# Two graph-attention layers: when the accumulator sums may start, where they stand against the mask extraction, and when a maximum is spread

## The chip, the core and the metric

The kernel runs on one core of a Trainium2 chip. The metric is device time in microseconds (us) from start to end of one execution, and the time of a kernel is the median of several runs. The engines of the core are TensorE (PE), VectorE (DVE), ScalarE (ACT), GpSimd (POOL) and SyncE (SP). Each works through its own instructions in the order in which they are written, and engines wait for one another with semaphores: an instruction adds to a semaphore when it is done, and another engine waits until the count has reached a value. A waiting instruction holds back all that stands behind it on its engine.

## The reference

Two layers of graph attention over 4096 nodes with 64 features, each with a residual and a layer norm. `adj` is a 4096 x 4096 matrix of 0 and 1.

```python
def _L0_gnn_ref(h, adj, a):
    src, dst = h @ a[:D, 0], h @ a[D:, 0]
    e = src[:, None] + dst[None, :]
    e = jnp.where(e > 0, e, 0.01 * e)
    attention = softmax(jnp.where(adj > 0, e, NEG_INF), axis=1)
    return attention @ h

def _L1_gnn_ref(h, adj, W, a):
    Wh = h @ W
    e = leaky_relu((Wh @ a1)[:, None] + (Wh @ a2)[None, :], 0.2)
    attention = softmax(jnp.where(adj > 0, e, NEG_INF), axis=1)
    return elu(attention @ Wh)

x = _layernorm(x + _L0_gnn_ref(x, adj, L0_gnn_a))
x = _layernorm(x + _L1_gnn_ref(x, adj, L1_gnn_W, L1_gnn_a))
```

## The kernel before

Since the exponential of a leaky ReLU of s + d is a product of a factor of the row and a factor of the column on either side of s + d = 0, the kernel never forms the scores. It forms two 0/1 matrices, "edge and s + d > 0" (`pos`) and "edge and s + d < 0" (`neg`), and multiplies each by weighted values (`wmov`). The row's factors are applied to the sums afterwards.

**Tiling.** Each layer goes over 8 supertiles q of 512 rows, each of 4 tiles t of 128 rows. Inside a supertile stand 8 steps k, each over 512 columns in 4 blocks. I write (layer, q, k) for a step, so (1,3,0) is the first step of supertile 3 of layer 1. One step passes through four engines:

- ACT, `compare` (L666): four instructions write the signs of s + d for the step into `neg`, one of 4 buffers.
- DVE, `negative` (L827) and `positive` (L838): bitwise operations with the mask `mask_t` make `neg` and `pos`. There are 2 buffers of `pos`.
- PE, `products` (L1215): 32 matmuls, 8 for each tile t, that add into the accumulator `acc[t]` in PSUM. They wait for `positive` of the step. In the middle of a step, after tile 1, stands what the function `between` issues.
- In layer 0 the mask must first be made: PE transposes a piece of the loaded `adj` into `tb` (L1139, in `between`, two steps ahead), and DVE extracts it from there (`extract`, L753, one step ahead). The transpose for a later step waits until `tb` is extracted. Layer 1 uses the same masks again. The pieces of `adj` are loaded by DMAs that POOL issues, each when its buffer has been transposed.

**The end of a supertile.** After step 7 the four accumulators are read by `sum_parts` (DVE, L853): four reductions, one for each tile, into `part`. They stand behind `positive` of step 0 of the next supertile. Sum t waits until PE has finished tile t (`acc_ready`, for the last tile `mm_done`). The first product of step 0 into `acc[t]` waits for sum t (`acc_free`). Then the epilogue runs on POOL: two instructions (L341, L343) multiply `part` by the row factors, and these two are the only ones that read `part`. The rest (L346 to L417) works in `num`, `tmp` and small columns up to the write of `xout` (L417). On its way it needs DVE twice (a reciprocal; `take_stats`, L867 and L871) and in layer 1 ACT once (`elu`, L647, an exponential that stands behind the signs of step 5). `pdone[layer]` counts its instructions, `EPI` = 13 in layer 0 and 17 in layer 1 for each supertile. In layer 1 `take_stats` stands ahead of `negative` of step 7, so the epilogue ends shortly before the next supertile's sums.

**The sums' wait.** `sum_parts` waits until the whole epilogue of the supertile before has counted (L845, L847). It guards `part`, which the new sums overwrite.

**The maximum.** In (0,6) the maximum of the column terms of layer 1 is spread to all partitions: DVE takes it over columns (`find_max`, L761), PE transposes it (`turn_stat`, L1155), DVE takes it over the row (`spread_max`, L766), PE spreads it (`spread_stat`, L1159), and DVE copies it (`take_max`, L778) and centres the column terms (`centre`, L772). From these ACT makes exponentials (L601, L602, behind the signs of step 3), from which POOL makes the first weights of layer 1 (L328, written behind its epilogue's step 2 work), and DVE and ACT finish them in (0,6) and (0,7). Both PE instructions stand ahead of the products of (0,6,1).

The loops over q: supertiles 0, 1, 6 and 7 of each layer are written out, 2 to 5 run in a hardware loop of two supertiles a turn.

## Time and profile before

| | |
|---|---|
| median of 3 runs | 445.18 us (444.62 to 447.87) |
| the profiled execution, whole | 445.9 us |
| its span, first to last instruction | 444.3 us |
| PE busy | 409.0 us, 92% |
| ACT busy | 383.4 us, 86% |
| DVE busy | 379.6 us, 85% |
| POOL busy | 252.9 us, 57% |

The span is one execution seen by the profiler. Layer 0 fills it up to about 243 us, layer 1 the rest. The engines are busy for 85% and more each, so the shares tell little of which one sets the pace. That must be read at the places where one waits for another.

### The profile page before, as it was taken

To read this page: it belongs to the slowest core of one execution; us is meant where nothing else is said; L and a number is where in the kernel's file an instruction comes from. 1 tells how busy PE (TensorE), PEld (TensorE's weight loads), DVE (VectorE), ACT (ScalarE), POOL (GpSimd) and SP (SyncE) were. 2 spreads that over 40 slices of the span, in tenths; PEclk is the share of its full clock that TensorE was granted. 3 is DMA by queue.
4 is the path that set the end of the run, shared out by engine and by line. 5 is a ranking of instruction groups with operands and counts; after the bars stand their busy time and mean duration, and the time that the engine had idled before them with its cause. 6 is when DMAs were issued, how large, how long until landed. Compare 5 with 4: busy or idle time off the path is not lost.

```text
span 444.3 us, 11835 instructions
## 1 busy us (share of the span) xinstructions
PE 409.0 (92%) x4484; PEld 396.8 (89%) x4484; DVE 379.6 (85%) x682; ACT 383.4 (86%) x590; POOL 252.9 (57%) x293
## 2 busy tenths in 40 slices
PE   1599999999999999999998989999999999999990
PEld 1388899999999999999998989999998999999980
DVE  4799898898989989889899988689898989898963
ACT  3898897979979798797998989999999898989930
POOL 5533263763737547295492135567786959595930
PEclk9999999999999999999999999999999999999995
DMA  5999979799897998989510000000000000000000
GB/s 114 97 107 107 90 68 96 63 101 84 74 101 60 98 88 70 88 73 87 78 52 1 1 25 2 1 25 2 26 1 25 0 24 0 24 1 24 3 25 16
DMA packets 22766, 22.48 MB, mean 51 GB/s; under 512 B 1344, under 2 KB 22464, under 8 KB 22720
## 3 DMA queue, kind: packets, MB, share of 16 engines
q0 software_dynamic: 17424, 16.78, 43.5%
q1 hardware_dynamic: 4208, 4.05, 2.8%
q10 hardware_dynamic: 1088, 1.05, 0.7%
q8 instruction: 28, 0.46, 0.4%
q14 instruction: 18, 0.15, 0.1%
HBM read 69.30 MB, written 2.10 MB: 161 GB/s over the span
## 4 chain that ended last, share of the span: by engine, by line
PE 40%; DVE 28%; issue 12%; ACT 9%; POOL 5%; DMA 3%; DVEq 1%; POOLq 0%; ACTq 0%
PE acc L1215 34%; DVE neg L827 9%; ACT neg L666 9%; PE tb L1139 5%; DVE odd L738 5%; DVE pos L838 3%; DVE scr L853 3%; POOL small L403 2%; DVE mask_t L753 2%; DMA enc<-in_adj 2%; DVE split L810 1%; DMA mask_t<-in_x 1%; POOL scr L404 1%; DVE mask_t L810 1%; DVE bst L867 1%
## 5 line engine op out<-in xcount | busy, mean ns | idle before, releaser
L1215 PE MATMUL acc<-wmov,pos 128*128 128x195 bf16 x2016 | 358.6, 248 | 7.7 <-DVE scr L853 3.3
L666 ACT ACTIVATE neg<-srcb,dcol 128x512 int8<-128x512 f32 x512 | 357.5, 959 | 4.6 <-PE acc L1215 4.4
L1215 PE MATMUL acc<-wmov,neg 128*128 128x195 bf16 x2016 | 358.7, 249 | 0.0
L1215 PEld LDWEIGHTS acc<-wmov,pos 128*128 128x128 fp8e4 x2016 | 198.5, 98 | 15.6 <-issue 8.1
L1215 PEld LDWEIGHTS acc<-wmov,neg 128*128 128x128 fp8e4 x2016 | 197.5, 98 | 2.3 <-issue 1.3
L838 DVE TENSOR_TENSOR pos<-neg,mask_t 128x1024 uint16<-128x1024 uint16 x128 | 104.6, 817 | 14.0 <-PE acc L1215 0.9
L827 DVE TENSOR_TENSOR neg<-neg,mask_t 128x1024 uint16<-128x1024 uint16 x128 | 105.8, 827 | 11.8 <-ACT neg L666 8.9
L486 POOL DMA_DIRECT2D enc<-in_adj x31 | 24.7, 798 | 63.4 <-PE tb L1139 60.1
L753 DVE TENSOR_SCALAR mask_t<-tb 128x512 uint32<-128x512 uint32 (+1 forms) x64 | 43.8, 685 | 10.0 <-PE tb L1139 10.0
L1139 PE MATMUL tb<-ident,enc 128*128 128x128 f32 x256 | 39.3, 277 | 3.8 <-DMA enc<-in_adj 3.8
L738 DVE SCALAR_TENSOR_TENSOR odd<-mask_t,odd 128x1024 uint32<-128x1024 uint32 x32 | 38.8, 1213 | 0.0
L341 POOL TENSOR_TENSOR scr<-scr,acol 128x260 f32<-128x260 f32 x14 | 13.7, 976 | 38.1 <-DVE scr L853 38.1
L853 DVE TENSOR_REDUCE scr<-acc 128x130 f32<-128x390 f32 x60 | 29.7, 555 | 6.5 <-POOL xout L417 6.3
L1139 PEld LDWEIGHTS tb<-ident,enc 128*128 128x128 f32 x256 | 28.9, 142 | 4.5 <-DMA enc<-in_adj 4.0
L403 POOL TENSOR_TENSOR small<-small 128x4 f32<-128x4 f32 x14 | 19.4, 1383 | 1.2
L400 POOL TENSOR_SCALAR small<-mv 128x4 f32<-128x4 f32 x14 | 9.1, 652 | 19.1 <-DVE mv L871 18.9
L343 POOL TENSOR_TENSOR scr<-scr,acol 128x260 f32<-128x260 f32 x14 | 14.9, 1064 | 0.0
L328 POOL TENSOR_TENSOR split<-val,bcol 128x520 f32<-128x520 f32 x8 | 9.2, 1155 | 8.4 <-ACT bcol L602 7.8
L631 ACT COPY xt<-pg 128x256 f32<-128x256 f32 x8 | 3.0, 369 | 12.6 <-PE pg L1175 12.6
L362 POOL TENSOR_TENSOR scr<-scr 128x256 f32<-128x256 f32 x14 | 12.9, 920 | 1.1
L346 POOL TENSOR_TENSOR scr<-scr 128x260 f32<-128x260 f32 x14 | 12.7, 907 | 1.1
L417 POOL TENSOR_TENSOR xout<-scr,small 128x256 f32<-128x256 f32 x14 | 12.5, 889 | 1.1
(138 smaller groups left out, 300.5 us busy)
## 6 DMA issues: line engine op xcount, KB each, us to landing
enc<-in_adj POOLq DMA_DIRECT2D x31, 512.0 KB, 8.4
mask_t<-in_x ACTq DMA_DIRECT2D x4, 256.0 KB, 6.0
x_rows<-xout SPq DMA_DIRECT2D x8, 128.0 KB, 3.9
resid<-x_rows SPq DMA_DIRECT2D x8, 128.0 KB, 2.1
out<-xout SPq DMA_DIRECT2D x8, 128.0 KB, 1.7
wmov<-mask_t SPq DMA_DIRECT2D x2, 390.0 KB, 3.9
enc<-in_adj POOLq DMA_DIRECT2D x2, 256.0 KB, 8.6
resid<-in_a SPq DMA_DIRECT2D x1, 64.0 KB, 4.6
```

The source lines that it names most:

```text
L341: ops.tensor_tensor(num, part[:, :, 0, :], wide(acol[:, layer, 0, q, :], FD), ALU.mult)\
L343: ops.tensor_tensor(tmp, part[:, :, 1, :], wide(acol[:, layer, 1, q, :], FD), ALU.mult)\
L403: ops.tensor_tensor(rstd, var, mhalf, ALU.pow).then_inc(done, 1)
L486: nc.gpsimd.dma_start(enc8[:, u, :, :], adj_v[q, u]).then_inc(adj_landed[u], 16)
L666: ins = nc.scalar.activation(neg[:, k % SR, :, b], srcb[:, q % 2, :], ACT.Sign, bias=dcol[:, layer, c:c + 1])
L738: nc.vector.scalar_tensor_tensor(odd[:, :], mask_pairs[:, n, :], NOT_BINARY, odd[:, :], ALU.bitwise_and, ALU.bitwise_or).then_inc(looked, 1)
L753: nc.vector.tensor_scalar(mask_t[:, q, k, :, :], tb[:, :, :].bitcast(U32), WORD, None, ALU.bitwise_and).then_inc(masked, 1)
L827: nc.vector.tensor_tensor(neg16[:, k % SR, :], neg16[:, k % SR, :], bits, ALU.bitwise_and)\
L838: nc.vector.tensor_tensor(pos16[:, k % MR, :], neg16[:, k % SR, :], bits, ALU.bitwise_xor)\
L853: nc.vector.tensor_reduce(part[:, t, :, :], acc[t][:, 0:2 * WC].rearrange("p (s r c) -> p s c r", s=2, r=SPLIT), AX.X, ALU.add).then_inc(a ...
L1139: ins = nc.tensor.transpose(tb[:, t, :], enc[:, k // KP, t, k % KP * P:(k % KP + 1) * P], ident[:, :])
L1215: ins = nc.tensor.matmul(acc[t][:, side * WC:(side + 1) * WC], m[:, t * P:(t + 1) * P, b], wmov[:, c, side * WC:(side + 1) * WC], start=fi ...
```

## The change

Four edits, in one diff:

- The sums of a supertile no longer wait for the whole epilogue of the one before, but for its first two instructions (count + 2). In its place the epilogue's first instruction gets the wait for the end of the epilogue before. That epilogue runs on the same engine, but for the last supertile of layer 0, whose epilogue runs on DVE.
- `sum_parts` can do a part of the tiles. In the general body the sums of tiles 0 and 1 stand ahead of `extract` for the next step, and those of tiles 2 and 3 behind it. In layer 1 there is no `extract`, so that the four follow one another as before.
- `take_max` and `centre` in (0,6) move from step 1 to step 2 on DVE.
- `spread_stat` on PE moves from ahead of the products of (0,6,1) into their middle, behind the transposes.

```diff
@@ epilogue_sums
+            if layer == 1 and is_first(q):
+                eng.wait_ge(pdone[0], EPI[0] * NQ)
+            elif later(q):
+                eng.wait_ge(done, base)
             eng.wait_ge(acc_free, TI * (Q + 1))
@@ sum_parts
-            def sum_parts(layer, q, Q):
+            def sum_parts(layer, q, Q, tiles=range(TI)):
                 if layer == 1 and is_first(q):
-                    dve.wait_ge(pdone[0], EPI[0] * NQ)
+                    dve.wait_ge(pdone[0], EPI[0] * (NQ - 1) + 2)
                 elif later(q):
-                    dve.wait_ge(pdone[layer], EPI[layer] * q)
-                for t in range(TI):
+                    dve.wait_ge(pdone[layer], EPI[layer] * (q - 1) + 2)
+                for t in tiles:
@@ DVE body
                     negative(layer, q, k)
                     positive(layer, q, k)
+                    if done is not None and k == 0:
+                        sum_parts(*done, range(0, TI // 2))
                     if ahead(layer, q, k, 1):
                         extract(*ahead(layer, q, k, 1))
                     if done is not None and k == 0:
-                        sum_parts(*done)
+                        sum_parts(*done, range(TI // 2, TI))
@@ DVE body, layer 0, last but one supertile
                         if k == 1:
                             spread_max(1)
+                        if k == 2:
                             take_max(1)
                             centre(1, 0, NB * EARLY)
@@ PE between()
+                        if layer == 0 and is_last_but_one(q) and k == 1:
+                            spread_stat(1)
@@ PE body, ahead of products(0, 6, 1)
                         pe.wait_ge(grp_set, 3 * EARLY)
                         turn_stat(1)
-                        spread_stat(1)
```

How the order moves on DVE at the start of supertile (0,6), from its step 0 to the centring. The kernel before:

```order
L838 TENSOR_TENSOR pos<-neg,mask_t 128x1024 [waits negs,mm_done]
L753 TENSOR_SCALAR mask_t<-tb 128x512 [waits turned]
L853 TENSOR_REDUCE scr<-acc 128x130 [waits acc_ready,pdone0]
L853 TENSOR_REDUCE scr<-acc 128x130 [waits acc_ready] x2
L853 TENSOR_REDUCE scr<-acc 128x130 [waits mm_done]
L761 TENSOR_REDUCE stat<-dcol 128x1 [waits grp_set]
L827 TENSOR_TENSOR neg<-neg,mask_t 128x1024 [waits masked,signs]
L838 TENSOR_TENSOR pos<-neg,mask_t 128x1024 [waits negs,mm_done]
L753 TENSOR_SCALAR mask_t<-tb 128x512 [waits turned]
L766 TENSOR_REDUCE gst<-pg 1x1 [waits stat_turned]
L778 COPY cmax<-pg 128x1 [waits max_spread]
L772 TENSOR_SCALAR dcen<-dcol,cmax 128x20 [waits cmax_set]
```

The changed kernel at the same place (its lines are numbered a few higher: L857 is L853 of before, L757 is L753, L770 is L766):

```order
L842 TENSOR_TENSOR pos<-neg,mask_t 128x1024 [waits negs,mm_done]
L857 TENSOR_REDUCE scr<-acc 128x130 [waits acc_ready,pdone0]
L857 TENSOR_REDUCE scr<-acc 128x130 [waits acc_ready]
L757 TENSOR_SCALAR mask_t<-tb 128x512 [waits turned]
L857 TENSOR_REDUCE scr<-acc 128x130 [waits acc_ready,pdone0]
L857 TENSOR_REDUCE scr<-acc 128x130 [waits mm_done]
L765 TENSOR_REDUCE stat<-dcol 128x1 [waits grp_set]
L831 TENSOR_TENSOR neg<-neg,mask_t 128x1024 [waits masked,signs]
L842 TENSOR_TENSOR pos<-neg,mask_t 128x1024 [waits negs,mm_done]
L757 TENSOR_SCALAR mask_t<-tb 128x512 [waits turned]
L770 TENSOR_REDUCE gst<-pg 1x1 [waits stat_turned]
```

Two of the four sums have passed the extraction, and the copy of the maximum and the centring are gone from here. They stand one step later, behind the next `positive`, `extract`, the reciprocal and the copy of `scur`.

PE at the start of step (0,6,1), before:

```order
L1155 MATMUL pg<-ident,stat 1x128 [waits stat_set,grp_set]
L1159 MATMUL pg<-gst,ones 128x1 [waits gst_set]
L1215 MATMUL acc<-wmov,pos 128x195 [waits poss]
L1215 MATMUL acc<-wmov,neg 128x195
```

In the changed kernel L1162 (L1155 of before) is followed by the 16 products of tiles 0 and 1 (L1222). Behind them, in the middle of the step, stands this:

```order
L1146 MATMUL tb<-ident,enc 128x128 [waits masked,adj_landed1]
L1146 MATMUL tb<-ident,enc 128x128 x3
L1166 MATMUL pg<-gst,ones 128x1 [waits gst_set]
L1222 MATMUL acc<-wmov,pos 128x195
```

The matmul that spreads the maximum has moved from directly behind the transpose to 16 products and four mask transposes later.

## Rows read from the trace of the kernel before

**Rows 1.** Waits of all engines: who, line, for whom: us, times, longest

```profile
DVE scr L853 <- POOL xout L417: 6.3, 5, 1.3
PE acc L1215 <- DVE scr L853: 3.3, 7, 0.9
```

**Rows 2.** Timeline, PE, layer 1: start us, duration, instruction, [idle before]

```profile
292.60 0.24 PE L1215 MATMUL acc<-wmov,pos 128*128 128x195 bf16 x1
...
312.41 0.25 PE L1215 MATMUL acc<-wmov,pos 128*128 128x195 bf16 x1
...
315.10 0.25 PE L1215 MATMUL acc<-wmov,neg 128*128 128x195 bf16 x1
315.66 0.24 PE L1215 MATMUL acc<-wmov,pos 128*128 128x195 bf16 x1 [0.31 <-DVE scr L853]
...
412.59 0.26 PE L1215 MATMUL acc<-wmov,pos 128*128 128x195 bf16 x1
```

**Rows 3.** Timeline, DVE, supertiles (1,2) and (1,3)

```profile
291.11 2.25 DVE L853 TENSOR_REDUCE scr<-acc 128x130 f32<-128x390 f32 x4
293.28 0.68 DVE L827 TENSOR_TENSOR neg<-neg,mask_t 128x1024 uint16<-128x1024 uint16 x1
...
311.55 0.69 DVE L838 TENSOR_TENSOR pos<-neg,mask_t 128x1024 uint16<-128x1024 uint16 x1
...
314.95 1.98 DVE L853 TENSOR_REDUCE scr<-acc 128x130 f32<-128x390 f32 x4 [1.30 <-POOL xout L417]
316.84 0.68 DVE L827 TENSOR_TENSOR neg<-neg,mask_t 128x1024 uint16<-128x1024 uint16 x1
...
336.58 0.69 DVE L838 TENSOR_TENSOR pos<-neg,mask_t 128x1024 uint16<-128x1024 uint16 x1
```

**Rows 4.** Timeline, POOL, epilogues of (1,1) ending and (1,2) beginning

```profile
314.20 0.61 POOL L417 TENSOR_TENSOR xout<-scr,small 128x256 f32<-128x256 f32 x1
317.00 1.00 POOL L341 TENSOR_TENSOR scr<-scr,acol 128x260 f32<-128x260 f32 x1 [2.19 <-DVE scr L853]
```

**Rows 5.** Timeline, ACT and DVE, step (1,3,6): what the epilogue holds back

```profile
326.26 4.91 ACT L666 ACTIVATE neg<-srcb,dcol 128x512 int8<-128x512 f32 x7
...
329.94 1.22 DVE L827 TENSOR_TENSOR neg<-neg,mask_t 128x1024 uint16<-128x1024 uint16 x1
```

**Rows 6.** Timeline, PE, layer 0: into (0,4) and into (0,6)

```profile
133.56 0.25 PE L1215 MATMUL acc<-wmov,neg 128*128 128x195 bf16 x1
133.93 0.24 PE L1215 MATMUL acc<-wmov,pos 128*128 128x195 bf16 x1
...
187.60 0.25 PE L1215 MATMUL acc<-wmov,neg 128*128 128x195 bf16 x1
187.81 0.24 PE L1215 MATMUL acc<-wmov,pos 128*128 128x195 bf16 x1
```

**Rows 7.** Timeline, DVE, start of supertile (0,6)

```profile
186.50 0.69 DVE L753 TENSOR_SCALAR mask_t<-tb 128x512 uint32<-128x512 uint32 x1 [1.13 <-PE tb L1139]
187.11 1.97 DVE L853 TENSOR_REDUCE scr<-acc 128x130 f32<-128x390 f32 x4
```

**Rows 8.** Timeline, PE, start of step (0,6,1)

```profile
191.01 0.27 PE L1155 MATMUL pg<-ident,stat 128*1 128x128 f32 x1
191.66 0.38 PE L1159 MATMUL pg<-gst,ones 1*128 1x1 f32 x2 [0.37 <-DVE gst L766]
191.97 0.26 PE L1215 MATMUL acc<-wmov,pos 128*128 128x195 bf16 x1
```

**Rows 9.** Timeline, ACT, supertile (0,6): exponentials, signs, and a later wait

```profile
192.53 0.22 ACT L601 ACTIVATE bcol<-dcen 128x20 f32<-128x20 f32 x1 [0.51 <-DVE dcen L772]
...
192.77 5.60 ACT L666 ACTIVATE neg<-srcb,dcol 128x512 int8<-128x512 f32 x8
...
207.47 0.37 ACT L631 COPY xt<-pg 128x256 f32<-128x256 f32 x1 [1.45 <-PE pg L1175]
```

**Rows 10.** Timeline, DVE, `negative` of step (0,6,4)

```profile
198.73 0.66 DVE L827 TENSOR_TENSOR neg<-neg,mask_t 128x1024 uint16<-128x1024 uint16 x1
```

## Prediction

> **What bounds the kernel now.** I read the waits first. Two of them belong together [rows 1]: DVE's sums waited 6.3 us in 5 places for the last instruction of the epilogue, and PE's products waited 3.3 us in 7 places for the sums. The second is small beside 444.3 us, so the question is whether PE is what sets the pace. It is: take PE's timeline of layer 1 [rows 2]. Supertile (1,2) starts its products at 292.60, its step 7 at 312.41, and its last product stands at 315.10. A product follows another at 0.09 (32 in the 2.78 from 312.41 on), so the next supertile could have begun at 315.19. An undisturbed supertile of layer 1 is thus 315.19 - 292.60 = 22.59 us. But (1,3,0) began at 315.66, and the reader sees the sums as its releaser.
>
> How much is lost in all? Without stalls (1,7,1) would begin four supertiles and one step after 315.19: 315.19 + 4 x 22.59 + 2.78 = 408.33. It began at 412.59 [rows 2]. So layer 1 loses 4.26 us between these points, more than the waits view puts down to the sums, because PE also pays at steps 1 and 7, where DVE is late by what it stood idle.
>
> DVE's timeline says why [rows 3]. At (1,2,0) the sums go straight through and take 2.25, stretched by PE, which is not yet done with the last tiles. At (1,3,0) DVE stands for 1.30 until L417 is done, which runs from 314.20 to 314.81 on POOL [rows 4], and only then sums for 1.98. From `negative` of (1,3,1) at 316.84 to the end of `positive` of (1,4,0) at 336.58 + 0.69 = 337.27 DVE has no idle time of note: 20.43 us of work. With the sums (1.98, the next instruction starts 0.09 before their end) this is 22.3 us, and with the 1.3 us of waiting 23.6. So PE could do a supertile in 22.6 and DVE in 22.3, but the wait makes it 23.6.
>
> In layer 0 each boundary has a stall too, another one [rows 6]: into (0,4) PE goes from 133.56 to 133.93, 0.28 more than the pace of 0.09. The cause is order on DVE [rows 7]: the extraction stands ahead of the sums and waits 1.13 us for PE's transposes. The sums start 0.6 us behind its start, and PE's first product 0.70 us after the first sum starts (187.11 to 187.81).
>
> **Part 1, the sums' wait.** The first two instructions of an epilogue start as soon as the sums are done (L341 at 317.00 behind sums that end at 316.93, [rows 3, 4]), so "count + 2" is reached early in a supertile and asked for only at the start of the next. The 1.3 us fall away in all 5 places. Take (1,3,0). Before, sum 0 started at 314.95 and PE at 315.66, 0.71 later. Now sum 0 can start 1.3 to 1.4 us earlier, near 313.6, and PE's tile 0 is free at about 314.3, ahead of 315.19. The last sum must wait for PE's last product, as in (1,2), where `negative` of step 1 follows 0.68 us after the first product (293.28 against 292.60). So DVE is held to PE from there, and every supertile looks like (1,2).
>
> Does DVE then keep up to step 7? In (1,2) it did, with 0.17 to spare: `positive` of step 7 ended at 311.55 + 0.69 = 312.24 and PE used it at 312.41 [rows 2, 3]. The DVE work between is the same in (1,3) to (1,6). This margin is about the hand-over itself, so a tenth may be lost per supertile. I take 4.2 of the 4.26 us. Bounds: nothing less than 3.7, if 0.1 to 0.15 is lost in each of four supertiles; nothing more than 4.3.
>
> What is late next? The wait that moved to POOL costs nothing, since POOL has done L417 itself 2.19 us before L341 may start [rows 4]. The epilogue starts earlier by what the sums gain, and so do the exponential on ACT behind it and the signs of step 6. In (1,3) those signs start at 326.26, four at 0.70 each (4.91 for 7), done about 329.1, and DVE takes them at 329.94 [rows 5]. Set against PE, which gained less than DVE there, the chain keeps some 0.3 to 0.8 us.
>
> One cost no row shows: sums that run beside L404 and L417 on POOL, since they waited for the latter so far. From below it is nothing; from above, if one blocked the other whole, 0.61 us (L417) in 5 places, 3.1 us. I take nothing, since that time would first fill the 2.19 us in which POOL waits. The Trainium skill (SBUF — State Buffer, Who interferes with whom) says that a `tensor_reduce` on this chip never contends with GpSimd for their shared port, but that an operation with two inputs in SBUF blocks or is blocked for the whole of the other. By that rule this cost is nothing and the gain of part 1 stays 4.2, where whole blocking would leave 1.1; no row of before can show it.
>
> **Part 2, two sums ahead of the extraction.** Now sum 0 follows `positive` and no longer waits for the transposes. In (0,6) the extraction idled 1.13 us from 185.37 on, so sum 0 starts near 185.4 and frees tile 0 near 186.1, long before PE is ready (187.60 + 0.09 = 187.69). The stall goes: 0.28 at the starts of (0,2) to (0,5), four times, and 0.12 at (0,6) and at (0,7), where the gap was 0.21 (187.60 to 187.81, [rows 6]). Sum: 4 x 0.28 + 2 x 0.12 = 1.4. The extraction comes behind two sums of 0.47 each. It stood waiting for 1.13 anyway, so it ends at most 0.1 to 0.3 later, and PE wants it only for the transposes in the middle of step 0, 16 products (1.4 us) after its start. At (0,1) DVE works without a break for the next two steps, so PE only stands later: no gain. From below the whole part is worth nothing, if PE's new time is taken by the next late mask or signs; from above 1.4 and some 0.5 at (0,1).
>
> **Part 3, the spreading.** Between (0,6,0) and (0,6,1) PE takes 191.97 - 191.01 = 0.96 us for two tiny matmuls, since the second waits for DVE's maximum [rows 8]. Now the first stays (nothing to its 0.27) and the second comes when its input is long there (nothing to 0.31, from 191.66 to 191.97). I take the middle of each, 0.15: the gain is 0.96 - 0.15 - 0.15 = 0.7, bounds 0.4 to 0.96.
>
> The price is on ACT. The centring comes a step later on DVE. A step takes 3.20 us there (187.81 to 191.01, [rows 6, 8]), and PE and DVE begin it some 0.8 sooner than before, so ACT's exponentials start at 192.53 + 3.2 - 0.8 = 194.9. Queued behind them are the signs of steps 4 and 5, which then start near 195.1 in place of 192.77, 2.3 us later [rows 9]. Queued behind them on DVE is `negative` of step 4, at 198.73 [rows 10]. The signs take 2.8 us (5.60 for 8), so they are done at 197.9, against 198.73 - 0.8 = 197.9 wanted: just hidden, since DVE then waits for transposes anyway. ACT gives the lateness back at its own later waits, 1.45 us ahead of L631 [rows 9] and others. What isn't hidden would be lost, up to some 0.5 us.
>
> **Sum.** 4.2 + 1.4 + 0.7 = 6.3 us, less 0.2 for small hand-overs and the extra register instructions in the loops. The profiled span goes from 444.3 to 438.2. The whole profiled execution took 445.9, 0.7 over the median of 445.18; I take the 6.1 off the median: 439.1.
>
> **Rivals.** Changes below 1%, or 4.45 us, are about what a measurement of this kernel can't tell from none.
>
> - *Layer 0 gives its part back.* The end of layer 0 and the start of layer 1 have stalls of their own, from weights that pass through POOL, ACT and DVE in turn. If one of these chains starts from something not moved by PE, parts 2 and 3 (2.0 us) vanish. For it: ACT is 2.3 us later in (0,6). Against: extraction and ACT's copies there wait for PE [rows 7, 9], so they shift with it. Time 445.18 - 4.1 = 441.1. Chance 0.15.
> - *DVE or the epilogue's chain stays the bound in layer 1.* The margins are 0.17 and 0.3 us. If 0.3 us is lost in each of 5 supertiles, the gain is 4.6 and the time 440.6. Chance 0.13.
> - *The epilogue chain becomes the bound, slower than before.* Place: POOL from L341 to the exponential and the signs of step 6 [rows 4, 5]. The price is what the chain grows by per supertile beyond its 0.3 us, five times. To eat 6.1 it must grow by over 1.5 us each; with 2 us each it would be 5 x 1.7 - 6.1 = 2.4 slower, 447.6. POOL gives no sign of it, since its instructions keep their neighbours on DVE but for the sums. Chance 0.03.
> - *The wait was not what held PE,* and the change does nothing in layer 1: 445.18 - 2.0 = 443.2. Against it stand the 4.26 us with the sums as releaser. Chance 0.05.
>
> The forecast has the rest, 0.64. The low end is all stalls gone, 4.3 + 1.9 + 0.96 = 7.2: 438.0. The high end takes in the first two rivals with a margin: 442.0. Faster by over 1% means below 440.7: the forecast and half of the second rival and a little of the first, 0.74. Slower by over 1%: 0.02. Within 1%: 0.24.
>
> **What would show it.** Sums of (1,3,0) to (1,7,0) without a wait for L417, and starts of PE's supertiles in layer 1 all 22.6 us apart. If they are 22.8 to 23.0 apart, with PE waiting at step 7 for `positive`, DVE is the bound; if DVE waits for signs at step 6, it is the epilogue's chain. In layer 0, no gap ahead of the first product of (0,2) to (0,7), and 0.3 us in place of 0.96 ahead of (0,6,1). If `negative` of (0,6,4) waits for ACT, part 3's price was not hidden. The prediction is wrong if POOL's instructions from L341 on become longer, or if PE's starts in (0,7) and (1,0) have not moved by what (0,6) gained.

## The result and the profile after

| | before | changed |
|---|---|---|
| median of 5 runs each, same chip | 445.26 us (444.62 to 447.87) | 438.74 us (438.66 to 442.47) |
| ratio | | 0.9854, 95% interval 0.9821 to 0.9887 |
| the profiled execution, whole | 445.9 | 442.47 |
| its span | 444.3 | 440.6 |
| PE busy | 409.0, 92% | 408.1, 93% |
| DVE busy | 379.6, 85% | 382.2, 87% |

The changed kernel is faster by 1.5%, 0.4 us under the forecast of 439.1. The profiled execution of the changed kernel happens to be its slowest: it reaches step (0,0,7) 2.2 us later than before does (50.12 us against 47.91), because of a slow stretch near the start that the last section shows. So I compare the two traces from the start of that step on. From there to the start of step (1,7,1) before takes 412.59 - 47.91 = 364.69 us (from the unrounded times), the changed kernel 408.64 - 50.12 = 358.52. That is 6.17 us less, where the forecast's three terms added up to 6.3.

The waits of the changed kernel, as [rows 1] of before (who, line, for whom: us, times, longest):

```profile
DVE scr L857 <- POOL xout L421: 0.2, 1, 0.2
PE acc L1222 <- DVE scr L857: 1.0, 2, 0.7
```

The sums' 6.3 us of waiting for the epilogue have become 0.2, and PE's 3.3 us for the sums 1.0. In the page's chain of what ended last, PE had 40% and DVE 28% in before:

```profile
PE 74%; DVE 12%; issue 5%; DMA 5%; POOL 1%; ACT 1%; DVEq 0%; POOLq 0%
```

PE's timeline of layer 1 (start us, duration, instruction), the first products of (1,2,0), (1,3,0) and (1,7,1), to be read with [rows 2]:

```profile
292.97 0.24 PE L1222 MATMUL acc<-wmov,pos 128*128 128x195 bf16 x1
...
315.56 0.24 PE L1222 MATMUL acc<-wmov,pos 128*128 128x195 bf16 x1
...
408.64 0.25 PE L1222 MATMUL acc<-wmov,pos 128*128 128x195 bf16 x1
```

A supertile takes 315.56 - 292.97 = 22.59 us, and so does each of the five, within 0.02: (1,2,0) to (1,7,1) is 115.67 us against 119.99 in before.

DVE and POOL where (1,3,0) begins, to be read with [rows 3, 4]:

```profile
313.34 0.69 DVE L842 TENSOR_TENSOR pos<-neg,mask_t 128x1024 uint16<-128x1024 uint16 x1
313.95 2.37 DVE L857 TENSOR_REDUCE scr<-acc 128x130 f32<-128x390 f32 x4
```

```profile
314.58 0.61 POOL L421 TENSOR_TENSOR xout<-scr,small 128x256 f32<-128x256 f32 x1
```

The sums start right behind `positive`, while POOL is still in its last instructions, and end 0.76 us after PE has begun the next supertile (316.32 against 315.56): they follow PE now, not POOL.

In layer 0 PE's rows at the start of (0,6) and around (0,6,1), to be read with [rows 6, 8]:

```profile
188.65 0.25 PE L1222 MATMUL acc<-wmov,neg 128*128 128x195 bf16 x1
188.74 0.24 PE L1222 MATMUL acc<-wmov,pos 128*128 128x195 bf16 x1
...
191.94 0.27 PE L1162 MATMUL pg<-ident,stat 128*1 128x128 f32 x1
...
193.96 0.38 PE L1166 MATMUL pg<-gst,ones 1*128 1x1 f32 x2
194.27 0.26 PE L1222 MATMUL acc<-wmov,pos 128*128 128x195 bf16 x1
```

The gap ahead of (0,6,0) is 0.09 us, the plain pace, and ahead of (0,6,1) only the first small matmul is left, 0.11 us (the product behind it starts at 192.05). In the middle of the step the second one holds the products for 0.31 us.

### The profile page after: what moved, and what is told of

Same layout as the page of the kernel before. It is cut to its first block, busy times and chain, and to the rows that moved or that the text cites. A ratio compares the mean times of both kernels' runs of the same rounds, so it can differ in the third digit from the quotient of the medians.

```text
span 440.6 us, 11844 instructions
## 1 busy us (share of the span) xinstructions
PE 408.1 (93%) x4484; PEld 399.5 (91%) x4484; DVE 382.2 (87%) x682; ACT 382.9 (87%) x590; POOL 254.4 (58%) x293
## 4 chain that ended last, share of the span: by engine, by line
PE 74%; DVE 12%; issue 5%; DMA 5%; POOL 1%; ACT 1%; DVEq 0%; POOLq 0%
PE acc L1222 66%; PE tb L1146 5%; DMA enc<-in_adj 3%; DVE neg L831 3%; DVE pos L842 2%; DMA mask_t<-in_x 1%; PE srcb L1156 1%; DVE mask_t L757 1%; DVE mask_t L814 1%; DVE split L814 1%; DVE wmov L820 1%; DVE scr L857 1%; ACT neg L670 1%; PE pg L1190 1%; DVE enc L814 1%
## 5 line engine op out<-in xcount | busy, mean ns | idle before, releaser
L1222 PE MATMUL acc<-wmov,pos 128*128 128x195 bf16 x2016 | 358.8, 249 | 5.0 <-DVE pos L842 3.8
L1222 PE MATMUL acc<-wmov,neg 128*128 128x195 bf16 x2016 | 358.9, 249 | 0.0
L1222 PEld LDWEIGHTS acc<-wmov,pos 128*128 128x128 fp8e4 x2016 | 199.1, 99 | 9.1 <-DVE pos L842 7.1
L1222 PEld LDWEIGHTS acc<-wmov,neg 128*128 128x128 fp8e4 x2016 | 198.1, 98 | 2.4 <-issue 1.3
L842 DVE TENSOR_TENSOR pos<-neg,mask_t 128x1024 uint16<-128x1024 uint16 x128 | 103.5, 809 | 14.1 <-PE acc L1222 0.9
L831 DVE TENSOR_TENSOR neg<-neg,mask_t 128x1024 uint16<-128x1024 uint16 x128 | 103.7, 811 | 11.6 <-ACT neg L670 9.1
L757 DVE TENSOR_SCALAR mask_t<-tb 128x512 uint32<-128x512 uint32 (+1 forms) x64 | 43.9, 686 | 8.2 <-PE tb L1146 7.4
L742 DVE SCALAR_TENSOR_TENSOR odd<-mask_t,odd 128x1024 uint32<-128x1024 uint32 x32 | 38.8, 1212 | 0.0
L857 DVE TENSOR_REDUCE scr<-acc 128x130 f32<-128x390 f32 x60 | 32.2, 558 | 2.0 <-POOL xout L421 0.2
L345 POOL TENSOR_TENSOR scr<-scr,acol 128x260 f32<-128x260 f32 x14 | 13.0, 927 | 30.0 <-issue 23.1
L404 POOL TENSOR_SCALAR small<-mv 128x4 f32<-128x4 f32 x14 | 8.9, 639 | 19.1 <-DVE mv L875 18.9
L328 POOL TENSOR_TENSOR split<-val,bcol 128x520 f32<-128x520 f32 x8 | 9.2, 1156 | 7.9 <-ACT bcol L606 7.8
L366 POOL TENSOR_TENSOR scr<-scr 128x256 f32<-128x256 f32 x14 | 13.1, 936 | 1.1
L374 POOL TENSOR_TENSOR scr<-scr,small 128x256 f32<-128x256 f32 x14 | 11.9, 850 | 2.1 <-DVE small L865 0.5
L421 POOL TENSOR_TENSOR xout<-scr,small 128x256 f32<-128x256 f32 x14 | 12.5, 891 | 1.1
```

The source lines that it names most:

```text
L742: nc.vector.scalar_tensor_tensor(odd[:, :], mask_pairs[:, n, :], NOT_BINARY, odd[:, :], ALU.bitwise_and, ALU.bitwise_or).then_inc(looked, 1)
L757: nc.vector.tensor_scalar(mask_t[:, q, k, :, :], tb[:, :, :].bitcast(U32), WORD, None, ALU.bitwise_and).then_inc(masked, 1)
L831: nc.vector.tensor_tensor(neg16[:, k % SR, :], neg16[:, k % SR, :], bits, ALU.bitwise_and)\
L842: nc.vector.tensor_tensor(pos16[:, k % MR, :], neg16[:, k % SR, :], bits, ALU.bitwise_xor)\
L857: nc.vector.tensor_reduce(part[:, t, :, :], acc[t][:, 0:2 * WC].rearrange("p (s r c) -> p s c r", s=2, r=SPLIT), AX.X, ALU.add).then_inc(a ...
L1222: ins = nc.tensor.matmul(acc[t][:, side * WC:(side + 1) * WC], m[:, t * P:(t + 1) * P, b], wmov[:, c, side * WC:(side + 1) * WC], start=fi ...
```

## The experiments

They ran on three chips in turn, each with its own runs of before: 446.56 us there for the first four kernels, 445.29 for the next four, 445.77 for the last three. A time is compared with its own before. Two traces are compared between the starts of the same steps on PE. These comparisons carry the argument: the runs of before on the first of the chips spread from 445.56 to 448.40 us, and by the medians there the three parts alone would bring 5.0, 2.5 and 0.4 us, more together than the whole change.

**One part at a time.** First the wait alone (edit of `epilogue_sums` and of the two waits in `sum_parts`, with the four sums in one piece):

```diff
-                    dve.wait_ge(pdone[layer], EPI[layer] * q)
+                    dve.wait_ge(pdone[layer], EPI[layer] * (q - 1) + 2)
```

> The kernel before with the sums' wait alone changed (count + 2, and the wait at the epilogue's first instruction); order on DVE and the spreading as before. My theory: it is the cause of nearly all that layer 1 gained, 4.3 us, so about 440.9 against 445.2, and PE's supertiles (1,2) to (1,7) start 22.6 us apart. The rival, that DVE gets its time in layer 1 from the order of the sums or from what layer 0 gained: under 3 us. Layer 0 should keep its gaps of 0.28 and 0.12 us.

Measured: 441.54 us, ratio 0.988 (0.9857 to 0.9903). PE's first product of (1,7,1), where that of (1,2,0) stands at 292.71:

```profile
408.38 0.25 PE L1219 MATMUL acc<-wmov,pos 128*128 128x195 bf16 x1
```

That is 115.67 us, to the hundredth what the changed kernel has, so all of layer 1's gain of 4.32 us is this edit. The starts in layer 0 are spaced as in before. Between (0,0,7) and (1,7,1) this kernel takes 360.40 us, 4.29 less than before.

Then the split of the sums alone, still behind the old wait:

```diff
+                    if done is not None and k == 0:
+                        sum_parts(*done, range(0, TI // 2))
                     if ahead(layer, q, k, 1):
                         extract(*ahead(layer, q, k, 1))
                     if done is not None and k == 0:
-                        sum_parts(*done)
+                        sum_parts(*done, range(TI // 2, TI))
```

> The kernel before with the order alone changed: sums of tiles 0 and 1 ahead of the extraction, 2 and 3 behind it; the old wait for the whole epilogue and the old spreading stay. My theory: 1.4 us, all in layer 0 (0.29 at the starts of (0,2) to (0,5), 0.12 at (0,6) and (0,7)), so about 443.8; nothing at (0,1). Layer 1 keeps its stalls, 4.3 us, with DVE waiting 1.3 us for L417 five times. The rival, that layer 0 gives its part back in (0,7) and (1,0): 445.2.

Measured: 444.1 us, ratio 0.9951 (0.9924 to 0.9978). The gaps ahead of (0,2) to (0,7) are gone on PE, 1.41 us in all. Layer 1's waits stand as they were: the view of the waits gives the first line of [rows 1] again, 6.3 us in 5 places. From (1,2,0) to (1,7,1) PE takes 120.03 us (119.99 in before).

The two parts act in different layers and don't touch each other.

Last the spreading alone:

```diff
+                        if k == 2:
                             take_max(1)
                             centre(1, 0, NB * EARLY)
@@ PE between()
+                        if layer == 0 and is_last_but_one(q) and k == 1:
+                            spread_stat(1)
@@ PE body, ahead of products(0, 6, 1)
-                        spread_stat(1)
```

> The kernel before with the spreading of the maximum alone changed on PE and DVE. My theory from the trace of the changed kernel: 0.84 us are gained ahead of (0,6,1) and 0.40 lost in its middle, so 0.4 to 0.5 us, about 444.8, which is near what can be told from none; the trace should show the two numbers. The rival: ACT's exponentials, now some 2 to 3 us later in (0,6), make the step (0,6,4) late, and it is 0 or a loss.

Measured: 446.12 us, ratio 0.9993 (0.9964 to 1.0022), no change. Its trace explains it. From (0,6,0) to (0,7,0) it takes 27.38 us against 27.82, so 0.44 is gained. From (0,7,0) to the start of layer 1 it takes 29.05 against 28.32, so 0.73 is lost again, more than was gained. I ran this kernel again, to see whether the loss is the luck of one execution:

> The third part alone a second time, in another execution. If the loss of 0.73 us behind (0,7,0), one stall of 2.1 us ahead of the products of (0,7,6), follows from the order and the times of this kernel, it stands there again, and the time is within 0.3 us of the kernel before. If it is the luck of one execution, how DVE and POOL meet, then the stalls at (0,7,5) to (0,7,7) are those of before (0.63, 0.34, 0.85), the way from (0,7,0) to (1,0,0) is 28.3, and the profiled execution is 0.4 below the kernel before at the same points.

Measured: 445.22 us, ratio 0.9987 (0.9969 to 1.0004). Every start on PE from (0,6,0) to (1,0,0) stands where it stood, within 0.01 us: 29.05 again. The loss belongs to the kernel. Rows of this trace, POOL's and then DVE's, from step (0,7,2) (which starts on PE at 220.78) on:

```profile
220.65 1.29 POOL L362 TENSOR_TENSOR scr<-scr 128x256 f32<-128x256 f32 x1
...
227.87 1.15 POOL L404 TENSOR_TENSOR scr<-scr,mv 128x256 f32<-128x256 f32 x1
...
230.00 1.52 POOL L328 TENSOR_TENSOR enc<-val,bcol 128x520 f32<-128x520 f32 x1
231.48 1.07 POOL L328 TENSOR_TENSOR split<-val,bcol 128x520 f32<-128x520 f32 x1
234.58 1.07 POOL L328 TENSOR_TENSOR enc<-val,bcol 128x520 f32<-128x520 f32 x1 [2.03 <-ACT wmov L622]
```

```profile
220.66 0.69 DVE L827 TENSOR_TENSOR neg<-neg,mask_t 128x1024 uint16<-128x1024 uint16 x1
...
227.85 0.70 DVE L816 TENSOR_TENSOR wmov<-split 128x520 bf16<-128x520 f32 x1
...
229.68 0.92 DVE L838 TENSOR_TENSOR pos<-neg,mask_t 128x1024 uint16<-128x1024 uint16 x1
...
231.56 1.55 DVE L810 TENSOR_TENSOR enc<-enc 128x520 f32<-128x520 f32 x1 [0.36 <-POOL enc L328]
...
234.62 1.57 DVE L838 TENSOR_TENSOR pos<-neg,mask_t 128x1024 uint16<-128x1024 uint16 x1
```

And the rows of before at the same instructions (PE starts (0,7,2) at 222.04):

```profile
221.91 0.73 POOL L362 TENSOR_TENSOR scr<-scr 128x256 f32<-128x256 f32 x1
...
228.90 0.61 POOL L404 TENSOR_TENSOR scr<-scr,mv 128x256 f32<-128x256 f32 x1
...
230.51 1.51 POOL L328 TENSOR_TENSOR enc<-val,bcol 128x520 f32<-128x520 f32 x1
```

```profile
221.92 1.27 DVE L827 TENSOR_TENSOR neg<-neg,mask_t 128x1024 uint16<-128x1024 uint16 x1
...
229.10 0.97 DVE L816 TENSOR_TENSOR wmov<-split 128x520 bf16<-128x520 f32 x1
...
231.20 1.37 DVE L838 TENSOR_TENSOR pos<-neg,mask_t 128x1024 uint16<-128x1024 uint16 x1
```

Read them so. At 220.65 a POOL instruction and `negative` on DVE start 0.01 us apart. With part 3 alone DVE runs its 0.69 and POOL takes 1.29. In before POOL ran its 0.73 and DVE took 1.27. Each time one of the two is done in its normal time and the other as if it had waited for the first. Up to L362 POOL stood equally far behind the start of (0,7,0) in both, to 0.01 us. The 0.56 us that L362 takes longer bring about a second meeting: L404 now starts 0.02 us behind `weigh`'s L816 on DVE and takes 1.15, where in before it started 0.20 ahead of it, ran its 0.61, and L816 took the longer time. So POOL reaches the weights' products (L328) 0.74 us later, at 230.00 - 214.38 = 15.62 against 230.51 - 215.63 = 14.88. In before, the first of these lies on `positive` of step 5 and lengthens it (1.37), and PE waits ahead of step 5. With part 3 alone it misses most of that one (0.92), but `weigh` (L810) must wait for it and then runs into the second (1.55), and `positive` of step 6 into the third (1.57, where in before it took 0.69). PE shows the outcome. From the product before to the first product of steps 5, 6 and 7 of (0,7) it takes 0.63, 0.34 and 0.85 us in before and 0.09, 2.08 and 0.39 here, where the pace is 0.09:

```profile
236.25 0.26 PE L1216 MATMUL acc<-wmov,pos 128*128 128x195 bf16 x1 [1.83 <-DVE pos L838]
```

The Trainium skill (SBUF — State Buffer, Who interferes with whom) says that an instruction of DVE with two inputs in SBUF contends with one of GpSimd that reads SBUF, and that who issues first keeps the port for its whole instruction. That one waits for the whole of the other agrees with these traces: 0.69 + 0.61 is about the 1.29. The order agrees for L404 and L816, of which the one that starts first keeps its time in both kernels. For L362 and `negative` the traces can't show it: POOL's recorded start is 3 to 7 ns ahead in all twelve traces that have this meeting, yet DVE is the one lengthened in before and with part 1 alone, and POOL in the ten others, each that has part 2 or part 3. What tips this tie stays open.

**Part 3 inside the change.** Does the changed kernel have this loss? Its way from (0,7,0) to (1,0,0) is 28.33 us, as in before. The same tie stands there (POOL takes 1.29), but L408, the L404 of before, takes 0.60, and L328 starts 14.89 us behind (0,7,0), as in before. The reason is part 2: its sums are done sooner, so the epilogue's chain on POOL stands 0.22 us nearer to the start of (0,7,0) (L366 starts 6.06 behind it, L362 of part 3 alone 6.28). L408 then starts at 13.29, ahead of `weigh` at 13.47, where part 3 alone had it at 13.50, behind. Part 2 alone shows the same 6.06 and 13.29. To see what part 3 is worth there, I took it back out of the changed kernel (the diff of part 3 above, reversed):

> The changed kernel without part 3: the maximum is copied and centred in step 1 of (0,6) again and both small matmuls stand ahead of the products of (0,6,1). My theory, that parts add up: (0,6,0) to (0,7,0) on PE is 0.44 us longer than in the changed kernel (27.82 against 27.38), with 0.96 us between the two first products there and nothing in the middle of step 1; from (0,7,0) to (1,0,0) 28.3 us, as before and as changed; the time is 439.4. Rival, what part 3 gained alone it loses later: (0,7,0) to (1,0,0) is shorter by 0.4 or more, and the time is 438.9 or less.

Measured: 439.14 us, ratio 0.9841 (0.9816 to 0.9866). (0,6,0) to (0,7,0) takes 27.70 us against 27.25 with part 3 (both 0.12 shorter than the figures expected, since the gap ahead of (0,7) is gone in both), and from there to layer 1 28.32. From (0,0,7) to (1,7,1) it takes 359.01 against 358.57 in a second execution of the changed kernel: 0.44 us. So within the change part 3 brings its 0.44 and nothing comes back, by the traces; the timed ratios are too close to tell. Ahead of (0,6,1) the second small matmul has its old wait of 0.37 us for DVE's maximum again.

**The price of the small matmul.** In the changed kernel the spreading matmul is issued twice:

```diff
+                if layer == 1:
+                    nc.tensor.matmul(pg[:, P:P + 1], ones[0:1, 0:1].broadcast_to([1, P]), gst[0:1, 0:1], start=True, stop=True)
                 nc.tensor.matmul(pg[:, P:P + 1], ones[0:1, 0:1].broadcast_to([1, P]), gst[0:1, 0:1], start=True, stop=True)\
```

> The changed kernel with the small matmul that spreads the maximum issued twice in the middle of (0,6,1), the same value to the same place. In the changed kernel it held the next product for 0.31 us. If each such fp32 matmul costs its own time on PE, the hold is near 0.5 to 0.6 us; if the 0.31 is mostly a change from the products to another shape and type and back, the second adds under 0.1 us and the hold is near 0.35 to 0.4. The rest of the kernel is unchanged, so the time moves by no more than 0.3 us.

Measured: 439.84 us in one run, which says little. PE's rows say it:

```profile
191.31 0.38 PE L1167 MATMUL pg<-gst,ones 1*128 1x1 f32 x2
191.55 0.36 PE L1168 MATMUL pg<-gst,ones 1*128 1x1 f32 x2
191.84 0.26 PE L1224 MATMUL acc<-wmov,pos 128*128 128x195 bf16 x1
```

The first takes 0.24 us up to the second, that one 0.29 up to the product: together 0.53 in place of 0.31. The step (0,6,1) is 0.22 us longer. So each such fp32 matmul of a single column costs some 0.22 to 0.24 us of its own, and the change of shape only the rest, under 0.1. This is read from one execution.

**Why half the sums.** In the changed kernel all four sums are put ahead of the extraction:

```diff
                     if done is not None and k == 0:
-                        sum_parts(*done, range(0, TI // 2))
+                        sum_parts(*done)
                     if ahead(layer, q, k, 1):
                         extract(*ahead(layer, q, k, 1))
-                    if done is not None and k == 0:
-                        sum_parts(*done, range(TI // 2, TI))
```

> The changed kernel with all four sums ahead of the extraction, none behind it. The last sum waits for PE's last product, and the extraction behind it would end about 1.3 us after PE's first product of step 0, where PE wants it 1.4 us after. If only the first sums matter to PE, the time is that of the changed kernel, 438.7, within 0.3. The rival, that the halving matters because the extraction becomes late for the transposes: a stall of PE in the middle of step 0 at (0,2) to (0,7), some 0.2 to 0.5 us each, so 440 to 441.5.

Measured: 444.06 us, ratio 0.9939 (0.9911 to 0.9967): most of the gain is gone (2.5 us are left against its own before). DVE's rows around the start of (0,2), which is at 79.37 us on PE, with two sums left out at the top:

```profile
78.88 1.26 DVE L857 TENSOR_REDUCE scr<-acc 128x130 f32<-128x390 f32 x2 [0.56 <-PE acc L1220]
80.05 0.68 DVE L757 TENSOR_SCALAR mask_t<-tb 128x512 uint32 x1
80.95 1.08 DVE L831 TENSOR_TENSOR neg<-neg,mask_t 128x1024 uint16<-128x1024 uint16 x1 [0.21 <-DVE mask_t L757]
82.13 1.04 DVE L842 TENSOR_TENSOR pos<-neg,mask_t 128x1024 uint16<-128x1024 uint16 x1
```

The same place in the changed kernel, where (0,2,0) starts at 81.81:

```profile
80.78 0.69 DVE L757 TENSOR_SCALAR mask_t<-tb 128x512 uint32 x1
81.39 1.18 DVE L857 TENSOR_REDUCE scr<-acc 128x130 f32<-128x390 f32 x2
82.48 0.68 DVE L831 TENSOR_TENSOR neg<-neg,mask_t 128x1024 uint16<-128x1024 uint16 x1
83.27 0.93 DVE L842 TENSOR_TENSOR pos<-neg,mask_t 128x1024 uint16<-128x1024 uint16 x1
```

The last sums must wait for PE's last products wherever they stand. In the changed kernel the extraction fills that time. With all four ahead DVE stands for 0.56 us, and the extraction comes behind, between the sums and `negative` of step 1, which moreover now waits 0.21 for it. `positive` ends 3.80 us behind PE's start of (0,2,0) in place of 2.39, and PE, whose step takes 3.20, starts (0,2,1) at 83.32, after 3.95. Not all of the 1.41 us by which `positive` is late is order. Some 0.9 is, and 0.51 comes from `negative` and `positive`, which take 1.08 and 1.04 in place of 0.68 and 0.93: they now meet the first instructions of POOL's epilogue (the second starts at 80.86 and takes 0.62, the third at 81.55 and takes 1.07). Without that PE would have lost about 0.2 a supertile in place of 0.75, by my estimate from these rows. The wait that I had feared, for the transposes in the middle of step 0, costs 0.08. 0.75 us are lost in each of (0,2) to (0,5) and 0.15 in (0,6), 0.18 is gained in (0,1), and (0,7,0) to (1,0,0) is 29.35 us, 1.0 longer. Between (0,0,7) and (1,7,1) it takes 362.56 us against 358.57, 4.0 more. I had not expected this: I took the extraction to be wanted only in the middle of step 0, and overlooked what is queued behind it on DVE.

**How much room DVE and the epilogue's chain have.** Two kernels add work to the changed one, beside the changed kernel itself:

> The changed kernel once more, as the measure for the three beside it. Expected 6.0 to 6.5 us under the kernel before. If its trace again shows PE late in (0,7,5) to (0,7,7) by 0.56, 0.26 and 0.76, the part of layer 0 is kept; if it shows the other pattern (one stall of about 2 us at (0,7,6), as in the kernel with the spreading alone), 0.7 us are given back and the pattern changes from one execution to the next.

Measured: 438.94 us, ratio 0.9854 (0.983 to 0.9879). From (0,0,7) to (1,7,1) the trace has 358.57 us, against 358.52 in the first one. PE is late beyond its pace at (0,7,5) to (0,7,7) by 0.55, 0.25 and 0.75: the part of layer 0 is kept.

A product on DVE ahead of `negative` of step 7, in each supertile of layer 1 that has an epilogue there (and once a constant to fill its tile):

```diff
+                            dve.wait_ge(padded, q)
+                            nc.vector.tensor_tensor(pad, pad, pad, ALU.mult).then_inc(padded, 1)
```

> The changed kernel with one needless instruction more on DVE in each supertile of layer 1 from (1,1) on, a 128x256 product of about 0.45 us, ahead of the negative of step 7. It leaves the result as it is. My theory: DVE has only the 0.17 us at step 7 to spare, so PE is late by about 0.3 us in each of (1,2) to (1,6), 1.4 us in all, 440.1 if the changed kernel is at 438.7. The rival, that DVE's work of 22.3 us against PE's 22.6 is what counts and step 7 recovers: 0.15 in each, 0.8 us; and if DVE were no bound at all: nothing.

Measured: 440.86 us, ratio 0.9892 (0.9868 to 0.9917). DVE and PE at step (1,2,7):

```profile
308.69 0.39 DVE L999 TENSOR_TENSOR enc<-enc 128x256 f32<-128x256 f32 x1
```

```profile
310.63 0.25 PE L1229 MATMUL acc<-wmov,pos 128*128 128x195 bf16 x1
```

The 0.31 us that the product holds DVE come out at PE as a start of 0.35 us behind the product before it, in place of 0.09, so 0.26 late, and the same in (1,2) to (1,5), 0.11 in (1,6): 1.19 us in all, between the theory's 1.4 and the rival's 0.8. (The medians differ by 1.9 us, with intervals of over 1 us each.) The margin of DVE at step 7 is what the rows said, about nothing: 0.31 less 0.26 leaves 0.05, so a tenth of work more would show.

An instruction on POOL ahead of the exponential's input:

```diff
+                ops.tensor_scalar(pad, pad, 0.0, None, ALU.min).then_inc(padded, 1)
                 ops.tensor_scalar(tmpf, numf, 0.0, None, ALU.min).then_inc(done, 1)
```

> The changed kernel with one needless instruction more on POOL in each epilogue of layer 1, a 128x256 minimum of 1.2 to 1.9 us, ahead of the input of ACT's exponential. It leaves the result as it is. It tells what room the epilogue's chain has: the signs of (1,4,6) end 0.8 us ahead of DVE's negative in the changed kernel. Rival of the prediction (the chain becomes the bound): ACT's signs of step 6 are late by 0.4 to 1.1 us in (1,3) to (1,6), DVE and then PE with them, 1 to 4 us in all. If the chain has more room than that, since DVE gets back time elsewhere: under 0.5 us.

Measured: 440.13 us, ratio 0.9882 (0.9855 to 0.9908). PE is late at step 7 by 0.21 us in (1,2) to (1,5), 0.86 in all. ACT and DVE in (1,4), first of this kernel, then of the changed kernel, whose trace is 2.15 us later there (338.13 against 335.98 at (1,4,0)): the exponential, the four signs of step 6 and the `negative` that takes them:

```profile
346.58 0.42 ACT L659 ACTIVATE scr<-scr 128x256 f32<-128x256 f32 x1 [0.46 <-POOL scr L387]
346.90 2.88 ACT L678 ACTIVATE neg<-srcb,dcol 128x512 int8<-128x512 f32 x4
...
349.97 1.22 DVE L839 TENSOR_TENSOR neg<-neg,mask_t 128x1024 uint16<-128x1024 uint16 x1
```

```profile
347.92 0.42 ACT L651 ACTIVATE scr<-scr 128x256 f32<-128x256 f32 x1
348.24 2.87 ACT L670 ACTIVATE neg<-srcb,dcol 128x512 int8<-128x512 f32 x4
...
351.91 1.22 DVE L831 TENSOR_TENSOR neg<-neg,mask_t 128x1024 uint16<-128x1024 uint16 x1
```

The added instruction (L386) takes 1.17 us, the one behind it 0.84 in place of 1.17, so the exponential waits for POOL and starts 346.58 + 2.15 - 347.92 = 0.81 us late, and the signs of step 6 end 0.82 late. They still end 0.19 us ahead of `negative` (349.78 against 349.97), where the changed kernel has 0.80. So the chain through ACT had about 0.8 us of room in (1,4) to (1,6), and this kernel uses it up: DVE still does not wait for the signs. (Behind the exponential POOL makes up most of it, since its next instruction takes 1.26 in place of 1.86.) What PE lost came through DVE, whose `odd` (L750, L742 of the changed kernel) beside POOL took 1.43 in place of 1.21 us, and that 0.21 stays up to step 7. From which length on the chain itself decides was not measured.

**What is left in layer 0.** From (0,0,7) on, the largest stall of the changed kernel in layer 0 is ahead of (0,1,1), 1.0 us beyond the pace, with 0.24 behind it at (0,1,2). (The next are 0.75 at (0,7,7) and 0.55 at (0,7,5).) DVE is busy there nearly throughout, for 7.4 of the 7.65 us from (0,1,0) to (0,1,2). Three pieces can go later: the mean, from step 0 to step 1; a sum for the residual's columns, from (0,1) to (0,0,7); the limits, to step 6.

```diff
@@ DVE, (0,0)
+                        if k == KB - 1:
+                            sum_s(2, 4, 3)
@@ DVE, (0,1)
-                        if k == 0:
+                        if k == 1:
                             take_mean(0)
-                        if k == 2:
+                        if k == 6:
                             dve.wait_ge(val_set, 2)
                             find_limits(0)
-                        if k == 1:
-                            sum_s(2, 4, 3)
```

> The changed kernel with three small instructions of DVE moved out of the start of (0,1), where PE still waits for DVE three times: the reduction of the mean (0.6 us) from step 0 to step 1, the sums of s for supertiles 2 and 3 (0.6) from (0,1,1) to (0,0,7), where DVE idles 1.17 us, and the limits (0.16) from step 2 to 6. My theory: PE's start of (0,1,2), set by this chain, comes 0.6 us sooner and nothing gives it back, so 0.5 to 0.6 under the changed kernel. The rival, that POOL's epilogue of (0,0) gets its mean too late and makes the stats of step 3 late: 0 or a loss.

Measured: 437.96 us, ratio 0.9838 (0.9813 to 0.9863), beside 438.94 for the changed kernel on the same chip. PE at the start of (0,1,1), where the second execution of the changed kernel stood for 0.84:

```profile
54.37 0.26 PE L1222 MATMUL acc<-wmov,pos 128*128 128x195 bf16 x1 [0.18 <-DVE pos L842]
```

Between (0,0,7) and (1,7,1) it takes 357.73 us against 358.57: 0.84 less, all of it before (0,2,0): 0.66 ahead of (0,1,1) and 0.24 ahead of (0,1,2), less 0.05 ahead of (0,1,0). The intervals overlap; the trace carries the claim. It is the fastest kernel of this study.

## Why the prediction was right, step by step

**Part 1: 4.2 forecast, 4.32 measured.** The step "Without stalls (1,7,1) would begin at 408.33" was the right one: from the pace of one undisturbed supertile, 22.59 us, the whole gain follows, while the waits view puts only 3.3 us on the sums, and that over both layers. I took off 0.06 for margins that turned out to be held: (1,2) to (1,6) take 22.57 to 22.59 us each. The cost that no row showed, sums beside L417, is nothing: the four sums around L421 at (1,3,0) take 0.55 to 0.56 us each, as those at (1,2,0) in before do, and L421 beside them took 0.61 us as L417 did [rows 4]. The added wait on POOL cost nothing, as forecast. The sign "POOL's instructions from L341 on become longer" did not come in layer 1, where the epilogues of (1,1) to (1,5) take 21.2 to 21.4 us from L345 to L421, as from L341 to L417 in before. It came in layer 0 with those of (0,1) to (0,4), 16.8 in place of 16.4 us. PE's steps beside them are not longer.

**Part 2: 1.4 forecast, 1.41 measured,** 0.31, 0.29, 0.29 and 0.29 at (0,2) to (0,5) and 0.12 at (0,6) and (0,7). Nothing was gained at (0,1), as forecast: the sums began 0.6 us sooner, and PE stood longer ahead of (0,1,1). The forecast had the right reason for the extraction's lateness being free, but the reason is wider than I wrote: it stands in the time in which DVE waits for PE's last tiles. That is why two sums ahead and two behind work. Four ahead cost 4 us, by my estimate above more than half of the 0.75 a supertile by new meetings with POOL.

**Part 3: 0.7 forecast, 0.44 measured.** The failing term is the price of the second small matmul. I set the two at 0.15 each, the middle of bounds. The first costs 0.11, and 0.84 is gained ahead of (0,6,1); the second costs the whole 0.31 of its upper bound, and with small gaps around it step (0,6,1) lasts 3.62 us in place of 3.22: 0.84 - 0.40 = 0.44. The row that I had [rows 8] already showed it: 0.31 from its start to the next product, at a time when its input had just come. Nothing in it was waiting, so no part of it could be hidden by having the input sooner.

The price on ACT came as worked out, or a little worse. The exponentials start late and the signs behind them with them, here on ACT and DVE (the forecast had 194.9 by the trace of before; the changed kernel's is 0.93 us later at (0,6,0), so 195.8 here):

```profile
196.18 0.22 ACT L605 ACTIVATE bcol<-dcen 128x20 f32<-128x20 f32 x1 [3.06 <-DVE dcen L776]
...
196.41 4.24 ACT L670 ACTIVATE neg<-srcb,dcol 128x512 int8<-128x512 f32 x6
```

```profile
199.32 0.68 DVE L831 TENSOR_TENSOR neg<-neg,mask_t 128x1024 uint16<-128x1024 uint16 x1
```

The exponentials are 0.35 us later than that, by operations of DVE that took longer than in before (last section). The four signs of step 4 end at about 199.28 and `negative` takes them at 199.32, where DVE's own work ahead of it is just done. PE's steps (0,6,2) to (0,6,7) last as long as before, so nothing of it was lost: "just hidden" was right, by a few hundredths.

**The rivals.** "Layer 0 gives its part back" did not happen in the changed kernel, but the experiment with part 3 alone shows that it was a real case: there 0.73 us were given back for a gain of 0.44. I had looked for a chain that doesn't move with PE; what did it was how POOL and DVE meet at their shared port. That the changed kernel escapes it is luck as far as the forecast goes: part 2 moves POOL's chain by 0.22 us, which I had not counted on. "DVE stays the bound in layer 1" had the right place and no loss; with 0.31 us of work more it comes true. "The epilogue chain" had more room than the 0.3 us of that rival's price: with one instruction more on POOL the exponential started 0.65 to 0.82 us later in (1,2) to (1,6), and DVE did not wait for the signs in any of them. "The wait was not what held PE" falls with the first experiment.

**The sum.** 4.32 + 1.41 + 0.44 = 6.17 us, which is the whole difference of the two traces between the points named above. Taken off the 445.26 of before it gives 439.1, and 438.74 was measured. The 0.2 us for hand-overs wasn't needed; together with part 1's surplus of 0.12 it balanced part 3's term, 0.26 too high. That the total comes within 0.1 us is luck in so far. What is left between 439.1 and 438.74 is within the spread of the runs.

## What to carry over

When several engines are busy for 85% and more, measure the length of one undisturbed round on the engine that should set the pace, and multiply: what a stall really costs includes the late steps behind it, which the waits view puts down to others. An instruction that an engine can do at any time belongs into the time in which that engine must wait anyway; of a group of instructions that wait for different things, put only those ahead whose input is there, and count what is queued behind. Moving an instruction away from its wait saves the wait, but not the instruction's own time, which the trace shows where it ran with its input just there.

## What the runs showed of the hardware that I had not expected

- **Where POOL and DVE meet, one pays in full, and the starts on record don't always tell which.** DVE's bitwise operations and POOL's products, both with two inputs in SBUF, started under 0.01 us apart: once DVE took 0.69 and POOL 1.29, once POOL 0.73 and DVE 1.27, with POOL's start ahead on record both times. In one kernel this moved a later chain by 0.74 us and changed which of its instructions met, though the gain that set it off was 0.44. A small gain can so be paid for in another place, the same in both executions of that kernel.
- **Small operations of DVE too.** In (0,6,2) of the changed kernel the copy of `scur` took 0.61 us (0.13 in before) and ended with POOL's L366, and the centring took 0.67 (0.24 in before) and ended with POOL's issue of a DMA (L366 runs from 194.63 to 195.36, the issue from 195.29 to 196.11):

```profile
194.76 0.61 DVE L804 COPY scur<-scol 128x4 f32<-128x4 f32 x1
...
195.47 0.67 DVE L776 TENSOR_SCALAR dcen<-dcol,cmax 128x20 f32<-128x20 f32 x1
```

  The ends fit (195.37 and 195.36, 196.14 and 196.11), but no run was made to take them apart, and the DMA issue is the weaker case: in before the copy ran whole inside such an issue in its 0.13, while in the changed kernel without part 3 the centring took 0.52 and ended 0.03 us behind a product of POOL, with no issue near. It cost nothing here, since PE did not wait for it.
- **An fp32 matmul of one column costs about 0.23 us of PE,** as much as 2.6 products of 195 columns at their pace of 0.09.
- **The start varies, with the clock's rise.** In the profiled execution of the changed kernel 36 products near the start stood 0.16 us apart, up to 27.4 us, in place of 0.09; in its second execution and in before there were 13. The view prints a granted clock of 1.00 (2.4 GHz) over this stretch, but the trace has no record of the clock there. Its first record, at 1.00, begins at 27.50 us in this execution, at 21.14 in the second and at 21.42 in before. In all 13 traces each product ahead of that first record stands 0.135 us or more ahead of the next, at a median of 0.16, and behind it the pace is 0.087. 195 columns in 0.163 us are 1.2 columns a nanosecond, which fits the lower of the clock's two levels (1.2 GHz). So I take it that the clock was at its lower level until then. The record doesn't say so itself, and why it rose later in this execution stays open. It is the main reason why this profile's span is longer than the timed median suggests:

```profile
26.43 0.37 PE L1222 MATMUL acc<-wmov,neg 128*128 128x195 bf16 x1
26.59 0.37 PE L1222 MATMUL acc<-wmov,pos 128*128 128x195 bf16 x1
```
